# Global attention: trial and score products in 64 by 64 quarters of the array, two units per step

## What is computed

```python
def _L1_attn_ref(x, Wq, Wk, Wv, Wu, bu):
    b, t, e = x.shape          # 2, 1024, 64
    h = HEADS                  # 8
    scale = e ** (-0.25)
    q = (x @ Wq).reshape(b, t, h, e) * scale
    k = (x @ Wk).reshape(b, t, h, e) * scale
    v = (x @ Wv).reshape(b, t, h, e)
    dot = jnp.einsum('bqhe,bkhe->bhqk', q, k)
    att = jax.nn.softmax(dot, axis=-1)
    out = jnp.einsum('bhqk,bkhe->bqhe', att, v).reshape(b, t, h * e)
    return out @ Wu + bu
...
t = t + _L1_attn_ref(_ln_t(t), L1_attn_Wq, L1_attn_Wk, L1_attn_Wv, L1_attn_Wu, L1_attn_bu)
```

## Time and profile before

| | us |
|---|---|
| median of three runs | 618.61 |
| span of the profiled execution | 618.9 |
| PE busy / DVE busy / ACT busy | 548.8 / 406.4 / 313.2 |
| first score product of the global attention | 176.13 |
| last value product of its loop ends | 491.1 |

### The profile page before, as it was taken

The page is one execution under the profiler, slowest core; times in us unless marked ns, Lnnn a source line. Parts: engine busy times, 40 slices in busy tenths (PEclk is TensorE's granted clock), DMA queues, the critical chain, the costliest instruction groups (busy, mean ns, idle before and its releaser), DMA issues.

```text
span 618.9 us, 10888 instructions
## 1 busy us (share of the span) xinstructions
PE 548.8 (89%) x4271; PEld 282.6 (46%) x4272; DVE 406.4 (66%) x740; ACT 313.2 (51%) x456; POOL 51.1 (8%) x106
## 2 busy tenths in 40 slices
PE   6999998998589999999999999999999833699962
PEld 5554654564134445444444454444444410266621
DVE  5545557467676656876887687776663457798753
ACT  2644445655036575555655556555656433465440
POOL 6030233212101000010000000000000000000000
PEclk9999999899669999999999999999999957899976
DMA  5000000000000000000000000000000000000001
GB/s 113 1 2 1 2 3 1 0 2 2 1 1 0 1 1 1 2 1 2 2 0 1 1 2 1 2 9 2 1 1 1 0 4 6 10 1 1 2 0 34
DMA packets 9513, 3.32 MB, mean 5 GB/s; under 512 B 8820, under 2 KB 9079, under 8 KB 9463
## 3 DMA queue, kind: packets, MB, share of 16 engines
q1 hardware_dynamic: 8182, 2.61, 1.9%
q10 hardware_dynamic: 1281, 0.01, 0.1%
HBM read 2.09 MB, written 0.52 MB: 4 GB/s over the span
## 4 chain that ended last, share of the span: by engine, by line
PE 79%; DVE 10%; issue 7%; ACT 2%; POOL 1%; POOLq 0%; DVEq 0%; ACTq 0%
PE PS L758 18%; PE PS L781 17%; PE PS L742 10%; PE PS L666 4%; PE PS L680 3%; PE PS L693 3%; PE PS L725 2%; PE PS L517 2%; PE PS L797 2%; PE PS L489 2%; PE PS L985 2%; PE PS L501 2%; PE PS L707 2%; DVE most L1547 2%; PE PS L563 2%
## 5 line engine op out<-in xcount | busy, mean ns | idle before, releaser
L1547 DVE TENSOR_REDUCE most<-PS 128x2 f32<-128x1024 f32 x128 | 156.6, 1224 | 76.7 <-PE PS L742 75.9
L1184 ACT ACTIVATE PT<-PS 128x1024 f32<-128x1024 f32 x128 | 131.0, 1024 | 98.7 <-PE PS L758 98.3
L758 PE MATMUL PS<-qS,aS 128*64 128x512 f16 x1024 | 133.9, 383 | 0.0
L781 PE MATMUL PS<-PT,V 128*64 128x512 f32 x512 | 130.8, 592 | 0.0
L742 PE MATMUL PS<-aS,qS 128*64 128x512 f16 x512 | 80.5, 395 | 10.6 <-DVE most L1547 10.4
L758 PEld LDWEIGHTS PS<-qS,aS 128*64 128x64 f16 x1024 | 56.7, 111 | 62.9 <-issue 28.2
L1140 ACT ACTIVATE prob<-sbias,negm 128x320 f32<-128x320 f32 (+1 forms) x64 | 34.3, 538 | 44.1 <-DVE negm L1593 43.8
L742 PEld LDWEIGHTS PS<-aS,qS 128*64 128x64 f16 x512 | 28.6, 112 | 42.0 <-DVE most L1547 18.5
L781 PEld LDWEIGHTS PS<-PT,V 128*64 128x64 f32 x512 | 36.0, 137 | 23.5 <-issue 0.9
L666 PE MATMUL PS<-ident 128*128 128x256 f16 x128 | 39.1, 306 | 7.3 <-DVE negm L1593 6.4
L1303 POOL TENSOR_TENSOR rstd<-var,minus_half 128x8 f32<-128x8 f32 (+1 forms) x9 | 13.5, 1505 | 357.8 <-DVE var L1411 357.8
(11 more groups left out here) (192 smaller groups left out, 670.5 us busy)
## 6 DMA issues: line engine op xcount, KB each, us to landing
xall<-in_x_dram SPq DMA_DIRECT2D x2, 256.0 KB, 4.4
out_dram<-x SPq DMA_DIRECT2D x4, 128.0 KB, 2.1
w<-in_L_attn_Wq_dram SPq DMA_DIRECT2D x2, 128.0 KB, 2.6
w<-in_L_attn_Wk_dram SPq DMA_DIRECT2D x2, 128.0 KB, 2.8
w<-in_L_attn_Wv_dram SPq DMA_DIRECT2D x2, 128.0 KB, 2.7
fc<-in_L_conv_fc_w_dram SPq DMA_DIRECT2D x2, 64.0 KB, 2.5
wu<-in_L_attn_Wu_dram SPq DMA_DIRECT2D x2, 64.0 KB, 2.4
w1s<-in_L_ffn_ffn_w_dram SPq DMA_DIRECT2D x2, 64.0 KB, 2.1
```

The costliest lines, as they stand in the source:

```text
L758: mm = pe.matmul(PS[h0:h0 + C, score_banks(t) + lane, :], aS[:, k0 + h0:k0 + h0 + C], qS[:, part, lane, toks], start=(part == 0), stop=(pa ...
L781: mm = pe.matmul(PS[cols, 6 + g % 2, :], V[:, img * NT + kt, cols], PT[:, g % 2, lane, kt, :], start=(kt == 0), stop=(kt == NT - 1))
L1184: act.activation(PT[:, g % 2, :, phase, :], PS[:, b0:b0 + 2, :], ACT.Exp).then_inc(c1["exped"], 1)
L1547: dve.tensor_reduce(most[:, g % 2, u // 2, u % 2, :], PS[:, 2:4, :], AX.X, ALU.max, negate=True)\
```

## The change

- `project` makes both lanes of a group in one go: lane 0 in the output's rows 0 to 63, lane 1 in rows 64 to 127, each once and not doubled. So `wqk` halves, one ACT copy and one DVE operation per group serve both heads, and 13 + 3 of each fall away. It stands at phase 4.
- `aX` (in the place of `kS[:, 1]`, used only in the routed part) is the input with its row halves exchanged, filled by two DMAs per image on the SP queue, after `drain_a`. The first trial of an image waits for them.
- `try_scores`: lane 0 on rows 0 to 63, lane 1 on rows 64 to 127, each with two column halves: four products in 64x64 quarters. Only the high part of the key input takes part.
- `scores`: four combinations of query part and input part, each in four quarters: sixteen products in place of eight.
- The PE program goes by two units: trial, two units of scores, trial, work beside the even unit, two units of values, work beside the odd unit. ACT and DVE programs keep their order unit by unit.

```diff
-        wqk = sb("wqk", [P, 2, NH1, 2, C], F16)
+        wqk = sb("wqk", [P, 2, NH1, C], F16)
...
+        aX = kS[:, 1, :]
...
-            def project(n, bank):
-                g, lane = PIECES[n]
+            def project(g, bank):
                 _, pair, blk, _ = group(g)
                 for part in range(2):
-                    for half in range(2):
-                        m = pe.matmul(bank[half * C:(half + 1) * C, :], wqk[:, part, pair * 2 + lane, half, :],
+                    for lane in range(2):
+                        m = pe.matmul(bank[lane * C:(lane + 1) * C, :], wqk[:, part, pair * 2 + lane, :],
                                       aS[:, blk * BLK:(blk + 1) * BLK], start=(part == 0), stop=(part == 1))
                 m.then_inc(piece_filled, 1)
+            def input_of(lane, part):
+                return (aS, aX)[lane ^ part][C * lane:C * lane + C, :]
             def try_scores(a):
@@ -734,13 +740,14 @@
                 if a:
                     pe.wait_ge(c1["tried_max"], a)
                 if u == 0:
-                    pe.wait_ge(piece_drained, 2 * (g + 1))
+                    pe.wait_ge(piece_drained, g + 1)
+                    pe.wait_ge(input_turned[img], 32)
                 q0 = toks.start + qt * P
                 k0 = img * TOK + half * BLK
-                for lane in range(2):
-                    for h0 in (0, C):
-                        mm = pe.matmul(PS[h0:h0 + C, 2 + lane, :], qS[:, 0, lane, q0 + h0:q0 + h0 + C],
-                                       aS[:, k0:k0 + BLK], start=True, stop=True)
+                for h0 in (0, C):
+                    for lane in range(2):
+                        mm = pe.matmul(PS[h0:h0 + C, 2 + lane, :], qS[C * lane:C * lane + C, 0, 0, q0 + h0:q0 + h0 + C],
+                                       input_of(lane, 0)[:, k0:k0 + BLK], start=True, stop=True)
                 mm.then_inc(c1["tried"], 1)
             def scores(t):
@@ -752,11 +759,12 @@
                 if t >= 2:
                     pe.wait_ge(c1["exped"], t - 1)
                 k0 = img * TOK + kt * P
-                for part in range(2):
-                    for lane in range(2):
-                        for h0 in (0, C):
-                            mm = pe.matmul(PS[h0:h0 + C, score_banks(t) + lane, :], aS[:, k0 + h0:k0 + h0 + C],
-                                           qS[:, part, lane, toks], start=(part == 0), stop=(part == 1))
+                for n, (q_part, k_part) in enumerate(((0, 0), (0, 1), (1, 0), (1, 1))):
+                    for h0 in (0, C):
+                        for lane in range(2):
+                            mm = pe.matmul(PS[h0:h0 + C, score_banks(t) + lane, :],
+                                           input_of(lane, k_part)[:, k0 + h0:k0 + h0 + C],
+                                           qS[C * lane:C * lane + C, q_part, 0, toks], start=(n == 0), stop=(n == 3))
                 mm.then_inc(c1["scored"], 1)
...
-            for t in STEPS:
+            def beside(t):
                 g, phase = divmod(t, NT)
-                if 0 <= t < UNITS:
-                    scores(t)
-                if 0 <= t + AHEAD < UNITS:
-                    try_scores(t + AHEAD)
-                if 0 <= t - LAG_VAL < UNITS:
-                    glob_values(t - LAG_VAL)
                 if 1 <= g <= NG and phase in (Y_PHASE, Y_PHASE + 1):
                     head_outputs(g - 1, phase - Y_PHASE)
-                n = 2 * (g + 3) + phase - PIECE_PHASE
-                if phase in (PIECE_PHASE, PIECE_PHASE + 1) and 6 <= n < 2 * NG:
-                    pe.wait_ge(piece_drained, n)
+                if phase == PIECE_PHASE and 3 <= g + 3 < NG:
+                    pe.wait_ge(piece_drained, g + 3)
                     if g >= 1:
                         pe.wait_ge(c1["y_drained"], 2 * g)
-                    project(n, small_bank(g))
+                    project(g + 3, small_bank(g))
                 if phase == SHIFT_PHASE and 0 <= g + 1 < NG:
                     if g < 0:
                         pe.wait_ge(c0["out_drained"], NTILE)
@@ -928,6 +928,26 @@
                 if t == ROW_T:
                     pe.wait_ge(shift_drained, 2 * (ROW_T // NT + 2))
                     show_row(small_bank(ROW_T // NT))
+            for t in STEPS:
+                if t % 2:
+                    if t == STEP0:
+                        try_scores(t + AHEAD)
+                        beside(t)
+                    continue
+                if 0 <= t + AHEAD < UNITS:
+                    try_scores(t + AHEAD)
+                if 0 <= t < UNITS:
+                    scores(t)
+                    scores(t + 1)
+                if 0 <= t + 1 + AHEAD < UNITS:
+                    try_scores(t + 1 + AHEAD)
+                beside(t)
+                for v in (t - LAG_VAL, t + 1 - LAG_VAL):
+                    if 0 <= v < UNITS:
+                        glob_values(v)
+                beside(t + 1)
...
-            def high_query(n, bank):
-                g, lane = PIECES[n]
-                act.wait_ge(piece_filled, n + 1)
-                act.activation(qS[:, 0, lane, group(g)[3]], bank, ACT.Copy, scale=1.0 / C).then_inc(piece_high, 1)
+            def high_query(g, bank):
+                act.wait_ge(piece_filled, g + 1)
+                act.activation(qS[:, 0, 0, group(g)[3]], bank, ACT.Copy, scale=1.0 / C).then_inc(piece_high, 1)
             drain_x(0, "x", 0)
...
-            def low_query(n, bank):
-                g, lane = PIECES[n]
+            def low_query(g, bank):
                 toks = group(g)[3]
-                dve.wait_ge(piece_high, n + 1)
-                dve.scalar_tensor_tensor(qS[:, 1, lane, toks], bank, 1.0 / C, qS[:, 0, lane, toks],
+                dve.wait_ge(piece_high, g + 1)
+                dve.scalar_tensor_tensor(qS[:, 1, 0, toks], bank, 1.0 / C, qS[:, 0, 0, toks],
                                          ALU.mult, ALU.subtract).then_inc(piece_drained, 1)
             def greatest(a):
@@ -1639,8 +1655,7 @@
...
-                if phase in (PIECE_PHASE + 1, PIECE_PHASE + 2) and 6 <= n < 2 * NG:
-                    low_query(n, small_bank(g))
+                if phase == PIECE_PHASE + 1 and 3 <= g + 3 < NG:
+                    low_query(g + 3, small_bank(g))
...
+            for img in range(B):
+                toks = slice(img * TOK, (img + 1) * TOK)
+                side_wait(sp, ("a", img, 1))
+                sp.dma_start(aX[C:P, toks], aS[0:C, toks]).then_inc(input_turned[img], 16)
+                sp.dma_start(aX[0:C, toks], aS[C:P, toks]).then_inc(input_turned[img], 16)
```

More of the change, by code:

```diff
@@ L282, in build @@
         normed = sem("normed")
+        input_turned = [sem(f"glob_input_turned_{img}") for img in range(B)]
         biased = sem("nat_residual_biased")
@@ L380, in build @@
         PIECE_STEPS = ((61, 62), (64, 65), (66, 67))
+        PIECE_BANKS = (2, 0, 1)
         TRY_STEP, STEP0 = 63, -5
@@ L452, in group @@
             return img, pair, img * NB + b, slice(g % 4 * BLK, (g % 4 + 1) * BLK)
-        PIECES = [(g, lane) for g in range(NG) for lane in range(2)]
         STEPS = range(STEP0, UNITS + 6)
@@ L1171, in _ @@
                     if i == at:
-                        for lane in range(2):
-                            high_query(2 * x + lane, PS[:, (2, 0, 0)[x] + lane, :])
+                        high_query(x, PS[:, PIECE_BANKS[x], :])
             def drain_state(img, bank):
@@ L1188, in _ @@
                        .then_inc(c1["out_drained"], 1)
-                n = 2 * (g + 3) + phase - PIECE_PHASE
-                if phase in (PIECE_PHASE, PIECE_PHASE + 1) and 6 <= n < 2 * NG:
-                    high_query(n, small_bank(g))
+                if phase == PIECE_PHASE and 3 <= g + 3 < NG:
+                    high_query(g + 3, small_bank(g))
                 if phase == SHIFT_PHASE and 0 <= g + 1 < NG:
@@ L1194, in _ @@
                     for lane in range(2):
-                        act.activation(qS[0:1, 0, lane, group(g + 1)[3]], small_bank(g)[C * lane:C * lane + 1, :],
-                                       ACT.Copy).then_inc(shift_drained, 1)
+                        act.activation(qS[C * lane:C * lane + 1, 0, 0, group(g + 1)[3]],
+                                       small_bank(g)[C * lane:C * lane + 1, :], ACT.Copy).then_inc(shift_drained, 1)
                 if t == TURN_T:
@@ L1641, in _ @@
                     if i == at:
-                        for lane in range(2):
-                            low_query(2 * x + lane, PS[:, (2, 0, 0)[x] + lane, :])
+                        low_query(x, PS[:, PIECE_BANKS[x], :])
                 if TRY_STEP <= i < TRY_STEP + AHEAD + STEP0:
```

15 lines of the change are left out of this document (6 added, 9 removed).

## The result

| | before | after |
|---|---|---|
| median of the timed runs, us | 619.65 (612.84 to 628.93, 20 runs) | 620.39 (619.03 to 636.47, 20 runs) |
| ratio after to before | | 1.0051, 95% interval 1.0027 to 1.0076 |
| span of the profiled execution, us | 618.9 | 617.3 |

The time is the same within two per cent; by the interval the change costs 0.3 to 0.8 per cent. In the changed kernel the lines are numbered anew: trial L749, scores L765, values L789, projection L727, ScalarE's copy of it L1142, VectorE's low part L1556, its reduce L1563, output products L805.

What follows compares the result with a forecast made beforehand. The prediction took PE to bound the global attention loop, busy 299.93 of 300 us. From 618.9 it added 3 for the loop and 6 for side work and took off 5 for the prologue: 623 us, range 612 to 632.

Steps and rivals of the forecast that it cites:

- Quarters: Trials and scores on PE: a round of four 64x64 quarters takes 0.215 us; one round per trial, four per scores.
- Rival (c): Four quarters don't run fully together on PE: rounds of 0.25 us, kernel at 645; chance 0.14.
- Change of tiles: PE switching between 64x64 and 128x64 tiles: 0.11 us each, kept at 0.09 to 0.16, paid twice a two-unit step.
- rival (b): A change of tiles on PE costs 0.05 us more, 0.16, giving 629; chance 0.12, half of it slower.
- Phases 2 and 3: Group step with the output products beside it: 4.99 us, with no wait of PE.
- Phases 4 and 5: Step with the projection: 5.71 us; second trial (B) 0.13 late, its reduce behind copy and low part, PE stalled 1.03.
- Phases 6 and 7: Step in which VectorE adds the outputs: 4.60 us, its second trial (B) 0.26 late.
- Group: Four steps of two units in the loop: 19.41 us against 19.15 before, +0.26; PE alone would give 18.0.
- Side work: VectorE's other loop work now stands before a reduce, at some twelve places, 0.5 us each: +6, between 2 and 9.
- Ahead of the loop: Prologue: seven one-round trials save 3.0 us, fewer low parts 1.9 at most; together -5, between -2 and -7.
- The copies of the input: Two DMA copies between row halves before the first trial: nothing added, at worst 0.6 us.
- Rival (a): VectorE's copies are covered after all and the time is PE's: 596 us; chance 0.15 for below 606.

Runs made afterwards that it cites:

- the unit-by-unit kernel: Kernel after the change, with PE's program put back to one unit at a time, quarters and single projection kept: 621.0 us, ratio 1.0029 to the kernel before.
- the first experiment: Kernel after the change, with VectorE's trial reduce put ahead of the low part in phase 5: 612.49 us, ratio 0.981 to the kernel before.
- The last experiment: Kernel after the change, with VectorE's reduce ahead of low part and side work, output additions one unit later, both weighings still ahead: 604.32 us, ratio 0.9833 to before.

## Why the prediction was right, and which terms were off

The forecast was 623, and the median is 620.39. The course was the predicted one: PE's gain given back to a reduce behind two copies. The sizes were less good: the loop was forecast 9 us longer and is 2.4 longer, and a group was forecast 0.26 longer and is 0.22 shorter. The sizes, by its own steps:

**Quarters.** A round was put at 0.215. The next instruction follows a trial by 0.24 (343.84 to 344.08, with the change in it), and a pair of units' scores takes 1.72 where 1.73 was predicted (339.93 to 341.65 in the rows below). Rival (c) is false; the 0.61 of L633 was no sign of halves that hinder each other. The Trainium skill, "TensorE: Matmul & The Clock Gate", section "Measured speedup vs the span model", lists four row tiles at 3.07 times one, from which the prediction estimated a round of 0.28. Four quarters took 0.215 here, no longer than two 64-column products side by side before. The page's figure is for another way to divide the array; for quarters the measurement decides.

**Change of tiles.** Put at 0.11 each, 0.22 a step. The timeline around phases 0 and 1:

```profile
339.69 0.40 PE L749 MATMUL PS<-aS,qS 64*64 64x512 f16 x1
...
339.93 0.38 PE L765 MATMUL PS<-qS,aS 64*64 64x512 f16 x1
...
341.65 0.38 PE L749 MATMUL PS<-aS,qS 64*64 64x512 f16 x1
...
341.97 1.94 PE L789 MATMUL PS<-PT,V 128*64 128x512 f32 x8
342.09 1.22 DVE L1563 TENSOR_REDUCE most<-PS 128x2 f32<-128x1024 f32 x1 [0.72 <-PE PS L749]
```

Out of the quarters: 341.65 + 0.215 = 341.87, and the values start at 341.97, 0.10. Into them: values end at 341.97 + 1.72 = 343.69, the trial starts at 343.84 and its round takes 0.02 more, 0.17. Together 0.27, and the unit-by-unit kernel shows the same. My figure was 0.05 a step too small, 3 us over 64 steps. The mean of the two, 0.135, is within the 0.09 to 0.16 that I kept; rival (b)'s 0.16 was half true.

**Phases 2 and 3.** Right: 5.04 for 4.99, the 0.05 being the changes.

**Phases 4 and 5.** The mechanism was right and the terms too large. Predicted 4.54 of work, B 0.13 late, and a stall of 1.03; measured 4.55 of work (the step of the first experiment), B not late, and 0.90 of stall. I had put 0.05 us between consecutive operations of DVE, which made 0.74 from the start of the low part to that of the reduce. The rows show 0.61 (352.45 to 353.06), less than the low part's own 0.69: that is the 0.13 of the stall. The rest of the chain came as predicted: projection to copy, copy to low part, and 1.27 from the reduce's start to the trial (1.28). The earlier trace rows already had no gap (354.35 + 0.69 = 355.04, the reduce at 355.02), so this much was to be read ahead of the result; that the overlap can reach 0.08 it does not show, since there the reduce started when its own trial was done.

**Phases 6 and 7.** Predicted 4.60 with B 0.26 late, measured 4.34 with B at 1.96: the same error, summed over the low part, the reduce and two additions.

**Group.** So 18.98, not 19.41: -0.22 to before where +0.26 was forecast, 5 us over twelve groups against the sum. PE alone was put at 18.0; with the order exchanged it is 18.09.

**Side work.** Put at +6, between 2 and 9. What the loop and its tail grew by, +3.3, less the groups' -2.6 and the rest's +0.2, is 5.7. So the term is of the right size, but not all of it is what it was put down for. The last experiment takes 2.9 back by order alone, and the later additions 1.1: that part is shown to be waiting behind a reduce. Another part is not VectorE's at all. After a function of image 1's MLP, ScalarE loads its table anew for the exponential, and PE's scores wait for it:

```profile
224.68 1.28 ACT L1202 ACT_TABLE_LOAD   x1
...
227.05 0.40 PE L765 MATMUL PS<-qS,aS 64*64 64x512 f16 x1 [1.65 <-ACT PT L1202]
```

The same wait stands in every kernel that goes by two units (1.65 with quarters, 1.49 without), also in those with the reduce ahead. It stands in none that goes by one unit, though the loads are there too: before (230.36) and in the unit-by-unit kernel (222.77). The prediction worked out only for phases 6 and 7 that the exponential ends in time, and had no term for this place. So the order of two units gave up cover on ScalarE as well.

**Ahead of the loop.** Put at -5, measured -3.6. Trials stand 1.97 apart in place of 2.39:

```profile
163.47 1.23 DVE L1563 TENSOR_REDUCE most<-PS 128x2 f32<-128x1024 f32 x1 [0.75 <-PE PS L749]
...
164.75 0.63 PE L749 MATMUL PS<-aS,qS 64*64 64x512 f16 x1 [1.33 <-DVE most L1563]
...
166.73 0.63 PE L749 MATMUL PS<-aS,qS 64*64 64x512 f16 x1 [1.33 <-DVE most L1563]
```

Seven of them are the -3.0 of the forecast; of the low parts' -2 some 0.6 came.

**The copies of the input** cost nothing. They were issued at 144.38 and 144.94, the page gives 2.3 us to landing, so they are there by 147.3; the first trial runs at 148.23, released by the low part.

```profile
kS<-aS SPq DMA_DIRECT2D x4, 128.0 KB, 2.3
```

**The whole.** With -3.6 and +3.3 the change comes to about -0.3 us in the profiled executions, where +4 was predicted; the other -1.3 lie ahead of it. By the medians it is +0.7, by the ratio's interval +1.7 to +4.7. Most of the way from the profiles to the medians is the choice of the execution: a run of the kernel before takes 1.8 us more than its span, so the profiled 618.9 stands for about 620.7 (an estimate), 1.1 above its median, while the profiled run of after, 619.42, is 1.0 below its own. Over all 20 executions of each kernel the means are 620.7 and 621.5, +0.8, so that the ratio's interval lies 1 to 4 us higher by the executions that it leaves out. Why one kernel's executions scatter stays open; the stage at 100 to 145 us is a place to look and no proof. That a forecast of 623 came within 3 us of 620.39 is in part luck: the loop was put 6.6 us too long, the stretch ahead of it 1.4 too short, and the difference of the medians is 2.3 above that of the profiled spans.

**Rival (a)**, 596 with the copies covered, is what the exchanged order makes true. It lacked the dearer changes: 64 steps by 0.05 bring it to 599, the wait for ScalarE's table (1.65) and the 1.4 less ahead of the loop to some 602. The last experiment's kernel has a profiled span of 601.0 and a median of 604.32.

## What to carry to other kernels

Before you let an engine issue two units at once, walk the other engines' program order through the same step: what stood behind a wait that used to be short may now stand in front of the operation that frees a single pair of banks, and exchanging two lines there was worth 12 us of 314, while the tiling with the old order of VectorE gained nothing, in either order of PE (313.4 and 314.4 against 312.0). Look at every engine that PE waits for: here a table load on ScalarE, which one unit at a time had covered, cost 1.65 us as well. Put the operation that releases a buffer ahead of everything on its engine that waits for something younger. Price a change of tile shape in both directions from the trace, and count it against a gain of the same size, as the 0.215 us of a round was against 0.27. And read the distance between starts, not the idle time in a row, for what a wait costs: 0.90 here, where the row says 0.83.

## What was not expected of the hardware

Four 64x64 products of 512 columns start within 0.01 us (343.84, .84, .85, .85) and the next round follows 0.215 us later, as after a pair of 128-row products before. A change into 64x64 tiles costs more (0.17) than one out of them (0.10). DVE's rows overlap: an operation starts up to 0.08 us before the one ahead of it has ended (353.06 against 353.14). And a stage ahead of the loop ran at a granted clock of 0.92 in some executions and 0.76 in others of the same kernel, while the loop behind it, at full clock, repeated to 0.2 us (314.4 and 314.2; 302.3 and 302.3).
